# Long cross attention: a ring of seven PSUM banks in place of three behind the last peaks

## The chip, the cores and the metric

One core of one Trainium2 chip. The metric is the time of one execution on the device, in microseconds. Engines: PE is TensorE (matrix multiply; PEld are its weight loads), DVE is VectorE, ACT is ScalarE, POOL is GpSimd, SP starts DMAs. Matmuls write into PSUM, which has 8 banks of 512 float32 per partition; DVE and ACT read results from there.

## The reference, cut to what matters

A decoder of two layers on `x` (32 x 56 x 128) with a context `ctx_1024` (32 x 1500 x 128). Each layer is attention, cross attention and a mixture-of-experts feed-forward, each added to `x` after a layer norm. The change is in the cross attention of layer 1: 16 heads of dimension 8, with rotary embedding of queries and keys, over 1500 keys:

```python
q = _rope((x_query @ Wq.T) split into heads, T_q)
k = _rope((x_kv @ Wk.T) split into heads, T_k)
v = (x_kv @ Wv.T) split into heads
attn = softmax(einsum('bhqd,bhkd->bhqk', q, k) * SCALE)
out = einsum('bhqk,bhkd->bhqd', attn, v)
return out.transpose(0, 2, 1, 3).reshape(B, T_q, DIM) @ Wo.T
```

## The kernel before, in words

Six stages (`l0_attn`, `l0_xattn`, `l0_ffn`, `l1_attn`, `l1_xattn`, `l1_ffn`) run one after another. Every engine has its own program, and semaphores tie the programs together. The fifth, `l1_xattn`, is "long cross attention"; in the profiled execution it runs from about 600 to 1327 us, and its last score step starts at 1318.31.

**How the fifth stage is tiled.** It goes through the batches b = 0 to 31. The 1500 keys of a batch are 12 tiles (`NK`) of 125 (`KT`). A step is a tuple such as `("score", b, kt)`. The kinds that matter:

- `peak` (12 for a batch): two matmuls (L2147) into a pair of banks, and one DVE reduction (L2261) that takes the greatest score. It gives the shift of the softmax.
- `shift`, `halve`, `rest`, `full`: DVE reduces the peaks to one number for each row (L2267), ACT casts it twice (L2345, L2349), DVE takes the rest (L2271), PE transposes it (L2155), and DVE adds it to the queries (L2278). Scores then come out already shifted.
- `score` (12 for a batch): eight matmuls (L2170), four into each of two banks. ACT takes the exponential of each bank (L2341, 125 x 448 elements) into one of four buffers `Pb`.
- `apply` (12 for a batch): 32 matmul instructions for two steps (L2186), values times exponentials, always into bank 3, where the sum of a batch builds up.
- `own`: ACT copies bank 3 (L2355) when a batch is complete. `fold` (PE L2195, DVE L2286 and L2289) transposes and divides by the sums. `turn` (PE L2201, ACT L2361) transposes again. `out` (PE L2207, DVE L2295) projects and adds to `x`, for two batches at once. `norm` and `finish` (POOL L127, DVE L143, PE L151, ACT L156) are the layer norm for the next stage.
- `keys`, `blend`, `high`, `low`, `values`, `fetch`, `write`, `stack`, `mask` prepare later batches. There are none from batch 30 on.

**Order.** `order()` (L1947) is one list, written out by hand, that all five engines walk through in turn; each engine does its own part of a step, so each engine's order is fixed. The core is, for n = 12 b + kt:

```python
yield ("score", b, kt)
...peak steps of b + 1 (kt < 6) or b + 2 (kt >= 6)...
yield from short        # full, fold, turn, out, finish at odd kt
if n >= 3 and n % 2:
    yield ("apply", *divmod(n - 3, NK)); yield ("apply", *divmod(n - 2, NK))
```

So scores and applies come in pairs, and the applies belong to the two steps before the pair of scores just issued. The last peak of all is `("peak", 31, 11)`, in the step of `("score", 30, 5)`. The next step in the list is the score of (30, 6); 18 score steps are left from there. The small steps among them are `full` of batch 31, `turn` 29, `out` 14, `own` 30, `fold` 30, `finish` 14 and `turn` 30, in this order, and at the very end `own`, `fold`, `turn`, `out`, `norm` and `finish` of the last batch.

**Banks.** The loop at L2002 gives every step its banks before the programs are built. Peaks alternate between the pairs 4, 5 and 6, 7. Bank 3 belongs to the applies. Scores (two banks) and all the small steps (one) take theirs from the ring 0, 1, 2 in the order of the list. On PE each step waits until its banks are free: `free[bank]` holds the mark of whoever reads the bank last, for a score the exponential (`exped`), for a fold the division, and so on. On ACT the exponential of step n waits for its scores and for the apply of step n - 4 (`applied`), because of the four buffers.

**Next stage.** `l1_ffn` begins on PE with the router's 16 small products (L2490), when the last row of the layer norm is in place, and goes on with the experts (L916, L928). Its weights are loaded from the point of `("score", 30, 0)` on.

Of the kernel before, what the change touches and what calls it, by code (L numbers as in the profile page):

```python
# [14 lines left out]
B, S, D, H = 32, 56, 128, 16  # L15
# [44 lines left out]
def decoder(nc, a, out):  # L60
    with ExitStack() as ctx:
# [1766 lines left out]
        def l1_xattn():  # L1828
# [118 lines left out]
            def order():  # L1947
                yield from (("clear", 0), ("mask", 0), ("mask", 1), ("keys", 2, 0), ("keys", 2, 1))
                for k in range(12):
                    yield ("peak", 0, k)  # L1950
                    if k in (1, 3, 5):
                        yield ("blend", 2, k // 2)
                    if k == 1:
                        yield ("keys", 2, 2)
                    if k in (6, 9):
                        yield ("high", 2, k // 3 - 2)
                        yield ("low", 2, k // 3 - 2)
                yield from (("shift", 0), ("halve", 0), ("rest", 0), ("full", 0), ("mask", 2), ("high", 2, 2), ("low", 2, 2))
                yield from (("write", 2, 0), ("write", 2, 1))
                for i in range(6):  # L1960
                    yield ("stack", 2, i)
                for k in range(6):
                    yield ("peak", 1, k)
                for n in range(B * NK + 2):
                    b, kt = divmod(n, NK)
                    if n < B * NK:
                        yield ("score", b, kt)
                        if kt < 6 and b + 1 < B:
                            yield ("peak", b + 1, 6 + kt)
                        if kt >= 6 and b + 2 < B:  # L1970
                            yield ("peak", b + 2, kt - 6)
                    steps = side(b)[kt] if n < B * NK else []
                    short = [x for x in steps if kt % 2 and x[0] in ("full", "fold", "turn", "out", "finish", "query")]
                    yield from short
                    if n >= 3 and n % 2:
                        yield ("apply", *divmod(n - 3, NK))
                        yield ("apply", *divmod(n - 2, NK))
                        if kt == 1:
                            yield ("own", b - 1)
                    yield from [x for x in steps if x not in short]  # L1980
                yield from (("fold", B - 1), ("turn", B - 1), ("out", NT - 1), ("norm", NT - 1), ("finish", NT - 1))
# [17 lines left out]
                    f += [("fetch", 3, ch) for ch in range(3)]  # L1999
                return f  # L2000

            at, ring, pair = {}, 0, 0  # L2002
            for step in order():
                if step[0] == "peak":
                    at[step] = 4 + 2 * (pair % 2)
                    pair += 1
                elif step[0] in ("score", "query"):
                    at[step] = ring % 3, (ring + 1) % 3
                    ring += 2
                elif step[0] in ("keys", "values", "full", "fold", "turn", "out", "finish"):  # L2010
                    at[step] = ring % 3
                    ring += 1

            for t in range(NT + 4):
# [503 lines left out]
        for k, f in enumerate((l0_attn, l0_xattn, l0_ffn, l1_attn, l1_xattn, l1_ffn)):  # L2518
            place.update(used=stages[4].parts["passing"] if k == 5 else 0, low=k % 2 == 0 or k == 5)
            stages.append(f())  # L2520
# [136 lines left out]
```

## Time and profile before

| what | us |
|---|---|
| runs shown: median | 1519.72 |
| lowest, highest of 3 | 1514.0, 1524.32 |
| profiled execution: its time | 1509.65 |
| profiled execution: span of the trace | 1507.9 |
| busy in the span: PE, DVE, ACT, POOL | 1352.3, 1105.7, 820.5, 784.4 |
| first score step behind the last peak starts at | 1295.11 |
| last apply of the stage ends at | 1320.58 |

The span runs from the first to the last instruction of the trace; 1.75 us of the execution's time lie around it. The trace is of one execution, at the low end of the runs. Times in the rows are microseconds from the start of the span, unless marked ns. PEclk is the granted clock of TensorE as a share of 2.4 GHz.

### The profile page before, as it was taken

The numbers are of one execution on the slowest core, as the hardware profiler recorded it, in microseconds if no ns is written. First come the engines' busy times: TensorE is split into PE (matmuls) and PEld (weight loads), VectorE is DVE, ScalarE is ACT, GpSimd is POOL, SyncE is SP. The second block draws the span as 40 slices with busy tenths as digits, with TensorE's granted clock in tenths as the row PEclk, the third lists the DMA queues.
The fourth block names the chain that finished last, engine by engine and source line by source line (L and its number), as shares of the span: only waits on it lengthen the run. The fifth ranks groups of instructions, "written<-read, shape, count | busy, mean of one in ns | idle before, by whom it ended". The sixth has DMA issues, their size and how long they took to land.

```text
span 1507.9 us, 41832 instructions
## 1 busy us (share of the span) xinstructions
PE 1352.3 (90%) x17179; PEld 923.6 (61%) x17179; DVE 1105.7 (73%) x1832; ACT 820.5 (54%) x1804; POOL 784.4 (52%) x736
## 2 busy tenths in 40 slices
PE   6888999999979985769999999999999999789998
PEld 4557888788946662436656665666666566555554
DVE  6885767757768878648888888888888888335554
ACT  3442344356623431537777777777777777723332
POOL 6675322424676666727777777777777772000000
PEclk9878999999989998879999999999999999989999
DMA  4004400026214034464644464454455454204230
GB/s 129 2 2 130 159 2 2 18 79 192 62 30 72 22 51 94 96 122 122 133 120 130 116 135 123 124 125 127 123 129 130 120 130 105 65 11 104 62 62 13
DMA packets 77088, 134.71 MB, mean 89 GB/s; under 512 B 18081, under 2 KB 56867, under 8 KB 73635
## 3 DMA queue, kind: packets, MB, share of 16 engines
q1 hardware_dynamic: 74850, 127.84, 34.4%
q0 software_dynamic: 2048, 4.20, 0.9%
q8 instruction: 137, 2.24, 0.7%
q14 instruction: 53, 0.43, 0.1%
HBM read 100.54 MB, written 34.73 MB: 90 GB/s over the span
## 4 chain that ended last, share of the span: by engine, by line
PE 42%; ACT 10%; DVE 5%; issue 3%; POOL 1%; DMA 1%; SPq 0%; ACTq 0%; POOLq 0%; DVEq 0%
PE ps L2186 11%; PE ps L916 7%; PE ps L2170 7%; ACT ARENA L2341 4%; PE ps L928 4%; PE ps L2133 3%; PE ps L2124 3%; PE ps L2147 2%; DVE ARENA L2261 2%; ACT ARENA L2319 2%; ACT ARENA L2325 2%; ACT ARENA L2332 1%; PE ps L2195 1%; PE ps L2155 1%; DVE ARENA L2271 1%
## 5 line engine op out<-in xcount | busy, mean ns | idle before, releaser
L2261 DVE TENSOR_REDUCE ARENA<-ps 112x2 f32<-112x1000 f32 x384 | 456.7, 1197 | 116.0 <-PE ps L2147 109.2
L2341 ACT ACTIVATE ARENA<-ps 125x448 f32<-125x448 f32 x768 | 378.3, 549 | 136.6 <-PE ps L2170 135.7
L2391 POOL TENSOR_TENSOR ARENA<-ARENA 64x500 f32<-64x500 f32 x192 | 227.8, 1187 | 109.2 <-ACT ARENA L2319 90.3
L2170 PEld LDWEIGHTS ps<-ARENA 64*125 64x125 bf16 x3072 | 122.6, 134 | 134.4 <-ACT ARENA L2341 71.6
L2170 PE MATMUL ps<-ARENA 64*125 64x112 bf16 x3072 | 169.4, 229 | 20.5 <-ACT ARENA L2341 19.3
L2186 PE MATMUL ps<-ARENA 125*17 125x112 f32 x6144 | 185.6, 262 | 0.0
L127 POOL TENSOR_TENSOR rs<-rs,mhalf 128x1 f32<-128x1 f32 x96 | 73.3, 765 | 178.9 <-DVE rs L122 178.6
L2147 PE MATMUL ps<-ARENA 64*112 64x500 bf16 x768 | 152.7, 387 | 10.0 <-DVE ARENA L2261 9.7
L2186 PEld LDWEIGHTS ps<-ARENA 125*17 125x17 f32 x6144 | 136.8, 98 | 32.2 <-issue 21.9
L2402 POOL TENSOR_TENSOR ARENA<-ARENA 128x500 bf16<-128x500 f32 x96 | 129.3, 1348 | 44.7 <-ACT ARENA L2325 44.7
L2397 POOL TENSOR_TENSOR ARENA<-ARENA 128x500 f32<-128x500 f32 x96 | 122.1, 1272 | 18.0 <-DVE ARENA L2254 11.8
L2124 PE MATMUL ps<-ARENA 128*128 128x500 f32 x192 | 107.3, 642 | 14.7 <-DMA ARENA<-in_ctxT 13.8
L916 PE MATMUL ps<-XT,ARENA 128*128 128x448 f32 x288 | 116.9, 550 | 0.0
L2133 PE MATMUL ps<-ARENA 128*125 128x128 f32 x768 | 110.2, 287 | 0.0
L2133 PEld LDWEIGHTS ps<-ARENA 128*125 128x125 f32 x768 | 93.4, 190 | 23.9 <-issue 22.3
L916 PEld LDWEIGHTS ps<-XT,ARENA 128*128 128x128 f32 x288 | 55.7, 195 | 53.6 <-issue 53.6
L2254 DVE TENSOR_TENSOR ARENA<-ARENA 128x500 f32<-128x500 f32 x96 | 83.3, 867 | 4.9 <-ACT ARENA L2319 4.9
L2319 ACT COPY ARENA<-ps 128x500 f32<-128x500 f32 x96 | 55.7, 581 | 48.1 <-PE ps L2124 44.1
L1009 DVE TENSOR_TENSOR ARENA<-ps,ARENA 128x448 f32<-128x448 f32 x72 | 44.9, 623 | 42.0 <-PE ps L916 40.9
L156 ACT COPY XT<-ps 128x128 f32<-128x128 f32 x96 | 25.6, 271 | 81.9 <-PE ps L151 81.7
L2325 ACT CAST ARENA<-ARENA 128x500 bf16<-128x500 f32 x96 | 58.5, 610 | 21.0 <-POOL ARENA L2397 15.2
L789 POOL TENSOR_TENSOR ARENA<-ARENA 128x896 f32<-128x896 f32 x16 | 27.0, 1690 | 81.1 <-DVE ARENA L718 81.1
(273 smaller groups left out, 2394.9 us busy)
## 6 DMA issues: line engine op xcount, KB each, us to landing
ARENA<-key_parts SPq DMA_DIRECT2D x192, 187.5 KB, 3.7
ARENA<-in_ctxT SPq DMA_DIRECT2D x96, 250.0 KB, 3.6
key_parts<-ARENA SPq DMA_DIRECT2D x64, 375.0 KB, 2.6
ARENA<-token_weights SPq DMA_DIRECT2D x16, 512.0 KB, 5.2
slots<-in_c_blank SPq DMA_DIRECT2D x2, 1472.0 KB, 12.5
results<-ARENA SPq DMA_DIRECT2D x42, 64.0 KB, 3.2
ARENA<-in_L_ffn_W SPq DMA_DIRECT2D x1, 2048.0 KB, 8.6
ARENA<-in_L_ffn_W SPq DMA_DIRECT2D x4, 512.0 KB, 10.3
```

What stands on the lines that cost most here:

```text
L916: e.matmul(ps[:, bk, 0:448], wt(x, c), rhs, start=True, stop=True).then_inc(up_mm.sem, 1)
L2124: e.matmul(ps[:, b1, 0:500], wk, C[b % 3][:, 500 * ch:500 * ch + 500], start=True, stop=True) \
L2133: m = e.matmul(ps[0:KT, b1, 128 * k:128 * k + 128], C[b % 3][:, KT * kt:KT * kt + KT], wv, start=True, stop=True)
L2147: m = e.matmul(ps[0:112, b1 + h, 0:500], Q0[r, b % 3, g].rearrange("p j s -> p (j s)"), KS[b % 4][r, g, 500 * ch:500 * ch + 500], start=Tr ...
L2170: m = e.matmul(ps[0:KT, b1[h], 112 * g:112 * g + 112], KS[b % 4][r, g, KT * kt:KT * kt + KT], Q1[r, b % 2, 112 * g:112 * g + 112], start=T ...
L2186: m = e.matmul(ps[32 * c:32 * c + 17, 3, 112 * u:112 * u + 112], V[b % 3][0:KT, kt, x, :], Pb[0:KT, n % NP_, 112 * x:112 * x + 112], start ...
L2261: e.tensor_reduce(mxp[0:112, b % 2, 2 * g:2 * g + 2, ch], ps[0:112, b1:b1 + 2, 0:500], AX, ALU.max) \
L2325: e.copy(Kh[:, 500 * ch:500 * ch + 500], T1[:, (3 * b + ch) % 3, :]).then_inc(k_hi.sem, 1)
L2341: e.activation(Pb[0:KT, n % NP_, 448 * h:448 * h + 448], ps[0:KT, b1[h], 0:448], ACT.Exp, bias=0.0, scale=1.0).then_inc(exped.sem, 1)
L2391: e.tensor_tensor(T2[r:r + 64, :], T0[64 - r:128 - r, n % 2, :], sin[64 - r:128 - r, sl], ALU.mult) \
L2397: e.tensor_tensor(T1[:, n % 3, :], T1[:, n % 3, :], T2, ALU.add).then_inc(k_sum.sem, 1)
L2402: e.tensor_tensor(Kl[:, sl], T1[:, (3 * b + ch) % 3, :], Kh[:, sl], ALU.subtract).then_inc(k_lo.sem, 1)
```

## The change

Only the giving out of banks changes. From the score step (30, 6) on, the ring starts anew with seven banks, 0, 1, 2, 4, 5, 6, 7; before it, everything is as it was. Peaks are no longer in the list then. No instruction is added, removed or moved in any engine's order.

```diff
-            at, ring, pair = {}, 0, 0
+            at, ring, pair, banks = {}, 0, 0, (0, 1, 2)
             for step in order():
+                if step == ("score", B - 2, 6):
+                    ring, banks = 0, (0, 1, 2, 4, 5, 6, 7)
                 if step[0] == "peak":
                     at[step] = 4 + 2 * (pair % 2)
                     pair += 1
                 elif step[0] in ("score", "query"):
-                    at[step] = ring % 3, (ring + 1) % 3
+                    at[step] = banks[ring % len(banks)], banks[(ring + 1) % len(banks)]
                     ring += 2
                 elif step[0] in ("keys", "values", "full", "fold", "turn", "out", "finish"):
-                    at[step] = ring % 3
+                    at[step] = banks[ring % len(banks)]
                     ring += 1
```

The scores from (30, 6) on get the banks (0,1), (2,4), (5,6), (7,0), (2,4), (5,6), then for batch 31 (0,1), (2,4), (6,7), (0,1), (2,4), (5,6), (0,1), (2,4), (6,7), (0,1), (2,4), (5,6). Before, they were (0,1), (2,0), (1,2), (0,1), (0,1), (2,0), then (2,0), (1,2), (1,2), (0,1), (2,0), (1,2), (1,2), (0,1), (0,1), (2,0), (1,2), (0,1). The small steps take the banks between: `full` 31 bank 1 (before 2), `turn` 29 bank 7 (1), `out` 14 bank 5 (0), `fold` 30 bank 7 (0), `finish` 14 bank 5 (2), `turn` 30 bank 7 (2), and at the end `fold`, `turn`, `out`, `finish` banks 0, 1, 2, 4 (0, 1, 2, 0).

## Rows read from the trace of the kernel before

**Rows 1.** Stretch, us; busy PE, PEld, DVE, ACT, POOL; clock, DMA share, GB/s.

```profile
1200.00:1250.00 50.00, 47.64 (x824) 31.05 (x818) 43.03 (x55) 38.10 (x87) 37.71 (x32) 1.00 0.61 129
...
1295.10:1320.60 25.50, 18.40 (x481) 14.42 (x477) 3.05 (x14) 18.47 (x42) 0.60 (x1) 1.00 0.01 3
...
1320.60:1326.70 6.10, 2.12 (x9) 1.10 (x9) 2.14 (x9) 1.08 (x4) 0.60 (x1) 0.91 0.00 0
```

**Rows 2.** Who waited for whom, 1295.1 to 1320.7: total, times, longest.

```profile
PE ps L2170 <- ACT ARENA L2341: 6.9, 9, 0.8
...
ACT ARENA L2341 <- PE ps L2170: 6.2, 15, 1.1
...
PEld ps L2170 <- issue: 5.0, 9, 0.9
```

**Rows 3.** Timeline, one pair of steps: start us, us, engine and line.

```profile
1307.51 0.43 PE L2170 MATMUL ps<-ARENA 64*125 64x112 bf16 x8 [0.72 <-ACT ARENA L2341]
...
1307.87 0.96 PE L2186 MATMUL ps<-ARENA 125*17 125x112 f32 x32
...
1308.76 0.44 PE L2170 MATMUL ps<-ARENA 64*125 64x112 bf16 x8
...
1309.29 0.98 ACT L2341 ACTIVATE ARENA<-ps 125x448 f32<-125x448 f32 x2 [0.37 <-PE ps L2170]
...
1309.98 0.43 PE L2170 MATMUL ps<-ARENA 64*125 64x112 bf16 x8 [0.78 <-ACT ARENA L2341]
```

**Rows 4.** Timeline, start of the stretch.

```profile
1295.11 0.44 PE L2170 MATMUL ps<-ARENA 64*125 64x112 bf16 x8
...
1295.16 0.35 DVE L2289 TENSOR_TENSOR ARENA<-ps,ARENA 56x64 f32<-56x64 f32 x2
...
1297.98 0.20 ACT L2349 CAST ARENA<-ARENA 112x8 f32<-112x8 bf16 x1
...
1298.22 0.18 DVE L2271 TENSOR_TENSOR ARENA<-ARENA 112x8 f32<-112x8 f32 x1 [2.62 <-ACT ARENA L2349]
...
1299.24 0.57 PE L2155 MATMUL ps<-ident,ARENA 112*128 112x112 f32 x4
```

**Rows 5.** Timeline, end of the stretch.

```profile
1318.85 1.73 PE L2186 MATMUL ps<-ARENA 125*17 125x112 f32 x64
...
1319.67 0.21 ACT L2361 COPY ARENA<-ps 128x56 f32<-128x56 f32 x1
...
1320.69 0.35 ACT L2355 COPY ARENA<-ps 128x224 f32<-128x224 f32 x1 [0.81 <-PE ps L2186]
```

**Rows 6.** A group of the page (mean ns), then ACT's timeline with no wait.

```profile
L2341 ACT ACTIVATE ARENA<-ps 125x448 f32<-125x448 f32 x768 | 378.3, 549 | 136.6 <-PE ps L2170 135.7
...
1216.53 0.99 ACT L2341 ACTIVATE ARENA<-ps 125x448 f32<-125x448 f32 x2
...
1217.39 0.21 ACT L2345 CAST ARENA<-ARENA 112x8 bf16<-112x8 f32 x1
...
1217.91 0.98 ACT L2341 ACTIVATE ARENA<-ps 125x448 f32<-125x448 f32 x2
```

**Rows 7.** Timeline, the small matmul steps within the stretch.

```profile
1305.04 0.49 PE L2207 MATMUL ps<-ARENA 128*128 128x128 f32 x2
...
1310.35 0.62 PE L2195 MATMUL ps<-ident,ARENA 128*56 128x128 f32 x4
...
1313.38 0.33 PE L151 MATMUL ps<-ident,xn 128*128 128x128 f32 x1
...
1318.65 0.27 PE L2201 MATMUL ps<-ident,ARENA 56*128 56x56 f32 x1
```

**Rows 8.** Busy time by half microsecond: fall and rise of the clock.

```profile
1325.50:1326.00 0.50, 0.11 (x1) 0.14 (x1) 0.25 (x1) 0.15 (x1) 0.00 (x0) 0.63 0.00 0
...
1339.00:1339.50 0.50, 0.50 (x3) 0.28 (x2) 0.00 (x0) 0.00 (x0) 0.00 (x0) 0.72 0.00 0
```

**Rows 9.** Timeline, a score step at half clock.

```profile
611.63 0.67 PE L2170 MATMUL ps<-ARENA 64*125 64x112 bf16 x8
```

## The prediction

> **What bounds the kernel now.** I read the table of busy time by stretch first. Only the end of the fifth stage can change: the new bank list begins with the seventh score step of the last but one batch, 18 steps before the stage's end. In the middle of the stage PE is busy 47.6 of 50 us. In the 25.5 us from 1295.1 it is busy 18.4, ACT 18.5, DVE 3.1, POOL 0.6, and the DMA queues 1% [rows 1]. Nothing is full, so this is a chain between two engines. The list of waits for the same stretch says which: the scores on PE waited for the exponentials on ACT 6.9 us in 9 waits, and the exponentials for the scores 6.2 us in 15 [rows 2].
>
> The timeline of one pair of steps shows it in full [rows 3]. Call a score step S, the two exponentials of a step E, one apply step A. S starts at 1307.51, the two applies at 1307.87, the next S at 1308.76, its E at 1309.29, and only at 1309.98, 0.69 after E began, comes the second S, with 0.78 idle before it that an exponential ended. Three banks explain it: a score takes two, so a second score needs a bank that the first score's first exponential has emptied. The pair takes 0.89 (applies) + 0.53 (S to E) + 0.69 (E to the second S) + 0.36 (second S to the next applies) = 2.47 us. Nine pairs are 22.2 us; the small steps between them bring the stretch to 25.5 us: from the first S at 1295.11 [rows 4] to the end of the last applies at 1318.85 + 1.73 = 1320.58 [rows 5].
>
> **The change part by part.** It adds and removes no instruction; it changes in which bank 18 score steps and the eleven small steps from there on land. Cost of the code itself: nothing. What can change is when a bank is free. I followed the seven-bank list by hand. The three banks at the seam are the ones used now for the first score (0 and 1). The second score gets 2 and 4: bank 2 is emptied by the division at L2289, which runs from 1295.16 for 0.35 us, so it can start at about 1295.6; bank 4 held the last peak but one. That delay of 0.1 us is hidden by a longer wait below. After that every score takes banks whose reader, in the schedule below, is finished 0.5 us or more before, so no score or small step waits for a bank. Bank 3, where the applies accumulate, is untouched.
>
> Without bank waits two sums compete. ACT: a step's two exponentials last 0.99 together, but the next instruction starts 0.86 after their start (1216.53 to 1217.39) [rows 6], so 18 steps are 15.5 to 15.7, and the small ACT steps 0.52 (two casts, 1217.39 to 1217.91 [rows 6]), 0.35 (bank 3's copy) and 0.21 twice [rows 5], and some 0.27 for the transposed row, together 1.5: 17.2. PE: a pair costs 0.36 + 0.36 + 0.89 = 1.61 by the starts in [rows 3], nine are 14.5; the small matmul steps have 0.57, 0.62, 0.49, 0.33 and twice 0.27 [rows 4, 7], each 0.07 shorter to the next start as S and A are, together 2.1; the last two applies another 0.9: 17.5. The engines are level, so the order decides. I worked the order out, step by step, t from 1295.11: S starts only after the PE's last work and costs 0.37; E starts 0.53 after S, 0.87 after the previous E, and when the apply four steps back is done; A (0.445) needs the end of both exponentials, 0.98 after E's start, and about 0.12 for the signal (bank 3's copy starts 0.11 after the last apply [rows 5]).
>
> S0 0, E0 0.53; S1 0.49, E1 1.40; two applies 0.9 to 1.75; S2, S3 to 2.5. Here stands the one wait that the banks don't touch: the transposes at L2155 need the halves of the shift, which ACT casts only after E1 (from 2.27; last cast 2.57 to 2.77) and DVE subtracts, 0.18 us (now it is 1297.98 + 0.20, then 1298.22 + 0.18 [rows 4]). So the transposes start at 3.05, not at 2.5. Then applies 3.56 to 4.45, S4 4.45, E4 4.98 (ACT idles 0.5), S5 and the turn, applies to 6.28, S6, S7; the projection waits for ACT's copy after E5 (6.72 + 0.21), 7.03 to 7.44; applies to 8.33; S8, S9; the next applies wait for bank 3's copy (8.64 + 0.35), 9.10 to 9.99; S10, S11, fold, applies to 12.17; S12, S13, one transpose, applies to 14.06; S14, S15, applies to 15.69; S16, S17, turn, two applies to 17.52, one to 17.97. E17 starts at 17.29 and ends, with the signal, at 18.39; the last apply ends at 18.84.
>
> Now it ends at 25.47. So the stretch loses 6.6 us. Where it goes: 9 waits of about 0.75 before the second S (6.9 in all) and the wait for ACT at the end (before it four applies lie behind the last E for 0.8 us, after it one), less about 0.5 at the transposes and 0.4 for bank 3. What is late next is the applies behind the exponentials, and ACT itself. Low end of this term: 3 us, if an issue gap stands before each score (below). High end: 25.47 less the larger engine sum of 17.5 is 8.0.
>
> Behind the stretch the path is serial and not touched: bank 3's copy at 1320.69 [rows 5], fold, turn, projection, norm, two transposes. Its 6.1 us have PE busy 2.1 [rows 1], and then the router's matmuls start the last stage. All the weights of that stage are in: the queues move 3 GB/s in the stretch. So nothing waits for a DMA if PE comes 6.6 us earlier: the queues have been still for 25 us by then.
>
> TensorE's clock is the unknown. It was granted in full all through the stretch, fell to half in the half microsecond from 1325.5, 5 us after PE's dense work ended, and rose in the one from 1339.0 [rows 8], so 13.6 us at 1.2 GHz lie on the path. The sparse 6.1 us remain as long as they are, so I expect a fall at about the same place. Price by rows: a score's matmuls take 0.67 at half clock against 0.44 [rows 9, 3], and half a duration is the most there is to win. If fall and rise move by 3 us against the work, 1.5 us either way. I take 0.
>
> The Trainium skill speaks against the change: "TensorE: Matmul & The Clock Gate", section "A second HAM failure mode: psum-queue depth-cycling", reports a kernel that went round PSUM banks each iteration, where short idle times between groups made the clock go down and up. By that rule a ring of seven could bring half clock into the stretch; here the ring of three already goes round, with 0.78 us idle in each pair, and the clock stayed full, so the trace disagrees so far, and I leave the sum as it is.
>
> Sum: 1509.65 (profiled execution; its span is 1507.9) - 6.6 = 1503.0. That execution lies 10 us below the median of the three runs, 1519.72, which is the basis for a forecast of a median: 1519.72 - 6.6 = 1513.1. The three runs spread from 1514.0 to 1524.3, more than the effect.
>
> **The rivals.**
> Issue, not banks: PE's weight loads before the scores have 5.0 us idle in 9 waits under "issue" [rows 2]. If part of the 0.8 us is the sequencer's own, more banks don't remove it. For it: that row. Against: at the same places the matmul row names the exponential, and the start comes 0.69 after E's start, 0.55 for one exponential [rows 6] and 0.14 for the signal. Price: 0.18 before each of 18 scores, on PE, is 3.2 us; gain 3.4, time 1516.3.
>
> Nothing happens: the exponentials' four output buffers, or the applies behind the exponentials, hold the pair at 2.47 us. For it: two scores, then two applies, all in order, is a tight loop. Against: in the schedule the apply that E needs is done 0.9 us or more before. Gain 0 to 1, time 1519.2.
>
> Slower: the clock falls to 1.2 GHz within the stretch. Place: the wait for the transposes at t = 2.5 and the start of the pairs. By the score rows the matmuls take 1.52 times as long: PE's 17.5 become 26.6, and with 0.9 of waits 27.5 against 25.5, so 2.0 us slower, 1521.7; twice as long would be 35.9, 10 us slower. It decides from 1.4 times on, where 17.5 + 0.9 reaches 25.5. For it: the clock does fall 5 us after the dense work ends [rows 8], and the start of the stretch keeps its waits. Against: they are 0.5 us each, and PE gets denser, not sparser.
>
> The clock's low stretch moves: PE is denser before the serial end, the fall comes elsewhere. 1.5 us either way around the forecast, no case of its own.
>
> **How the numbers follow.** Forecast (gain 4.5 to 8) 0.73; issue 0.15; nothing 0.08; half clock in the stretch 0.04. No case reaches 1% (15 us, about what a measurement of this kernel can tell from no change) by itself; only the spread of the runs could show one. So same 0.96, faster 0.03, slower 0.01. For the range I take the forecast's own 1511.7 to 1515.2, extend it by the two small-gain cases to 1519, and by the runs' spread of 4 to 5 us downwards: 1507 to 1520.
>
> **What would show it.** Right: the last applies end about 18.9 us after the first S of the stretch; consecutive S of a pair start about 0.37 apart; the waits of S for the exponentials vanish from the list and applies or transposes wait instead; ACT busy near 17.5 of 19; four consecutive exponentials 0.43 apart. Wrong: S still starts 0.69 after E (a bank is still held), or 0.18 and more before each weight load; a granted clock under 1.00 before 1314; the fold after bank 3's copy later than 1315.5.

## The result and the profile after

The changed kernel took 1505.31 us, the median of 11 runs (1502.43 to 1511.19). The kernel before, run again beside it, took 1514.15 (1509.12 to 1524.32, 11 runs, among them the three shown above). The ratio is 0.9936, with a 95% interval of 0.9911 to 0.9961: 9.7 us less, between 5.9 and 13.5. The two medians are 8.8 us apart. As forecast, the change stays under 1%. The forecast time was 1513.1, with 1507 to 1520: the measured median is 1.7 us below the range.

The profiled execution has a span of 1500.6 us against 1507.9 before. Line numbers from L2003 on are 2 higher than before. The same view as [rows 1], by stretch from the first late score to the last apply and on:

```profile
1295.40:1314.00 18.60, 16.94 (x481) 13.17 (x477) 3.06 (x14) 16.94 (x42) 0.60 (x1) 1.00 0.01 4
1314.00:1320.10 6.10, 2.30 (x9) 1.17 (x10) 2.15 (x9) 1.08 (x4) 0.60 (x1) 0.81 0.00 0
1320.10:1345.00 24.90, 24.90 (x75) 15.89 (x76) 11.02 (x28) 7.01 (x12) 0.95 (x1) 0.77 0.00 1
```

The same 481 matmuls and 42 ACT instructions now stand in 18.6 us instead of 25.5; both engines are 91% busy. The serial end, from the last apply to the router, is as long as it was, 6.1 us. The list of waits of that stretch, against [rows 2]:

```profile
PEld ps L2172 <- issue: 1.7, 9, 0.2
ACT ARENA L2343 <- PE ps L2172: 1.6, 2, 1.1
PEld ps L2188 <- ACT ARENA L2343: 1.1, 2, 0.5
PEld ps L2157 <- DVE ARENA L2273: 0.8, 1, 0.8
```

The 6.9 us that scores waited for exponentials are gone. "Issue" before the weight loads of the scores fell from 5.0 to 1.7 us, in 9 waits each time, but not the same nine. Before, five of them stood in front of the second score of a pair, 0.82 to 0.88 us each, 4.3 us together: that was the bank wait under another name, and these five are gone. The other four were 0.18 us in front of a first score. Now every one of the nine pairs has that 0.18 in front of its first score. Two rows of before and one of after, PE's weight loads:

```profile
1307.48 0.33 PEld L2170 LDWEIGHTS ps<-ARENA 64*125 64x125 bf16 x8 [0.82 <-issue]
...
1308.76 0.31 PEld L2170 LDWEIGHTS ps<-ARENA 64*125 64x125 bf16 x8 [0.18 <-issue]
```

```profile
1305.27 0.54 PEld L2172 LDWEIGHTS ps<-ARENA 64*125 64x125 bf16 x16 [0.18 <-issue]
```

Left are one wait of the transposes for DVE (0.64 us), one of the projection for ACT's copy (0.41), and two of the last applies for the exponentials (0.29 and 0.30). The timeline, first at the transposes, then one pair in the middle, then the end (to be read against [rows 3 to 5]):

```profile
1295.41 0.89 PE L2172 MATMUL ps<-ARENA 64*125 64x112 bf16 x16
...
1297.96 0.20 ACT L2351 CAST ARENA<-ARENA 112x8 f32<-112x8 bf16 x1
...
1298.19 0.18 DVE L2273 TENSOR_TENSOR ARENA<-ARENA 112x8 f32<-112x8 f32 x1 [2.30 <-ACT ARENA L2351]
...
1298.42 0.60 PE L2157 MATMUL ps<-ident,ARENA 112*128 112x112 f32 x4 [0.64 <-DVE ARENA L2273]
...
1302.47 0.46 PE L2209 MATMUL ps<-ARENA 128*128 128x128 f32 x2 [0.41 <-ACT ARENA L2363]
...
1304.23 5.47 ACT L2343 ACTIVATE ARENA<-ps 125x448 f32<-125x448 f32 x12
...
1304.38 0.96 PE L2188 MATMUL ps<-ARENA 125*17 125x112 f32 x32
...
1305.27 0.67 PE L2172 MATMUL ps<-ARENA 64*125 64x112 bf16 x16
...
1312.54 0.58 PE L2188 MATMUL ps<-ARENA 125*17 125x112 f32 x16 [0.29 <-ACT ARENA L2343]
...
1313.41 0.58 PE L2188 MATMUL ps<-ARENA 125*17 125x112 f32 x16 [0.30 <-ACT ARENA L2343]
...
1314.11 0.35 ACT L2357 COPY ARENA<-ps 128x224 f32<-128x224 f32 x1 [0.65 <-PE ps L2188]
```

Two scores are now one row of 16 matmuls in 0.67 us, where they were two rows 1.2 us apart. ACT runs 12 exponentials in 5.47 us without a gap. The last apply ends at 1313.41 + 0.58 = 1313.99, 18.58 us after the first late score; I had forecast 18.84.

So the traces differ by 25.47 - 18.58 = 6.9 us in this stretch. The rest of the 7.3 by which the spans differ is small: the stretch began 0.3 later, and everything behind the last apply took 0.7 less. The whole-run comparison, though, says 9.7. That difference, and where the median of the kernel before lies, is what the experiments are about.

### The profile page after: what moved, and what is told of

It is laid out like the page before. It is cut to its first block, busy times and chain, and to the rows that moved or that the text cites. A ratio compares the mean times of both kernels' runs of the same rounds, so it can differ in the third digit from the quotient of the medians.

```text
span 1500.6 us, 41822 instructions
## 1 busy us (share of the span) xinstructions
PE 1348.9 (90%) x17179; PEld 920.0 (61%) x17179; DVE 1106.9 (74%) x1832; ACT 819.2 (55%) x1804; POOL 781.2 (52%) x736
## 4 chain that ended last, share of the span: by engine, by line
PE 42%; ACT 10%; DVE 5%; issue 3%; POOL 1%; DMA 1%; SPq 0%; ACTq 0%; POOLq 0%; DVEq 0%
PE ps L2188 11%; PE ps L916 7%; PE ps L2172 6%; ACT ARENA L2343 4%; PE ps L928 4%; PE ps L2135 3%; PE ps L2126 3%; PE ps L2149 2%; DVE ARENA L2263 2%; ACT ARENA L2321 2%; ACT ARENA L2327 2%; ACT ARENA L2334 1%; PE ps L2197 1%; PE ps L2157 1%; DVE ARENA L2273 1%
## 5 line engine op out<-in xcount | busy, mean ns | idle before, releaser
L2172 PE MATMUL ps<-ARENA 64*125 64x112 bf16 x3072 | 167.4, 228 | 13.2 <-ACT ARENA L2343 12.3
```

The costliest lines, as they stand in the source:

```text
L2172: m = e.matmul(ps[0:KT, b1[h], 112 * g:112 * g + 112], KS[b % 4][r, g, KT * kt:KT * kt + KT], Q1[r, b % 2, 112 * g:112 * g + 112], start=T ...
```

## The experiments

I compare intervals within each trace, since the start of the fifth stage alone moves by over 20 us between the traces (607 to 630 us). "Late" is from the last peak's matmul to ACT's copy of bank 3; it is 1.9 us longer than from the first late score to the last apply.

**The changed kernel once more.**

> The changed kernel once more. Theory: the whole gain is the shorter stretch from the first score step behind the last peak to the last apply of the stage (25.5 us before, 18.6 after) and what follows is as long as before, so 7 us, a ratio of 0.9954 to the kernel before. The profile should show that stretch at 18.5 to 18.7 again. Rival: the medians are 8.8 us apart because something before the stretch got faster too; then the ratio stays at or below 0.9942 and the stretch begins earlier than at 1295.

1517.95 us against 1527.9 for the kernel before beside it, ratio 0.9938 (0.9918 to 0.9958). Late 20.4 us, as in the first trace. So the stretch repeats exactly (18.58 us from first score to last apply, as in the first trace), the ratio stays on the rival's side, and the rival's sign for it (the stretch begins earlier) can't be read from single traces: the last peak came at 1311 instead of 1294, since this set of runs was slower in the first stages.

**Four banks.**

```diff
-                    ring, banks = 0, (0, 1, 2, 4, 5, 6, 7)
+                    ring, banks = 0, (0, 1, 2, 4)
```

> The late ring has banks 0, 1, 2, 4 only. Theory: what cost time was that a pair of scores needs four banks and had three; with four the second score no longer waits for the first exponential, though some scores now wait for the exponential two steps back. Stretch 19.0 to 20.5 us. Rival (it takes the full seven to gain, since the small steps eat banks too): 22 us or more.

First late score 1314.02, last apply 1334.78, so 20.8 us, late 22.6. One bank more gives 4.7 of the 6.9 us, a little less than expected (19.0 to 20.5). In its list of waits the scores wait for exponentials again, but little:

```profile
PEld ps L2172 <- ACT ARENA L2343: 2.7, 9, 0.5
...
PE ps L2172 <- ACT ARENA L2343: 1.2, 3, 0.4
```

1.2 us in 3 waits against 6.9 in 9 [rows 2]. All three stand before the second score of a pair that no small step separates from the pair before. There the second score gets exactly the two banks of the score two steps back, as the theory said: (30, 9) gets 2 and 4, which the exponentials of (30, 7) have to empty first. Behind a small step, which shifts the ring by one, no score waits; but four of the small steps wait for an exponential themselves, 1.6 us in all. One row of each kind:

```profile
1316.55 0.44 PE L2172 MATMUL ps<-ARENA 64*125 64x112 bf16 x8 [0.38 <-ACT ARENA L2343]
...
1319.88 0.27 PE L2203 MATMUL ps<-ident,ARENA 56*128 56x56 f32 x1 [0.46 <-ACT ARENA L2343]
```

The remaining 2.2 us are what the seven are for.

**Only the small steps apart.** The scores stay on banks 0, 1, 2, the small steps go round 4 to 7. `late` becomes true at the score step (30, 6), where the changed kernel starts its new ring; that line of the edit is left out here.

```diff
-                    at[step] = banks[ring % len(banks)]
-                    ring += 1
+                    if late:
+                        at[step] = 4 + small % 4
+                        small += 1
+                    else:
+                        at[step] = banks[ring % len(banks)]
+                        ring += 1
```

> The scores keep banks 0, 1, 2; only the small matmul steps (full, fold, turn, out, finish) get banks 4 to 7 from the score step (30, 6) on. Theory: nothing gained, because the second score of each pair still waits for the first exponential: stretch 25.0 to 25.5 us. Rival (the small steps' share of the ring was the cost): 22 us or less.

27.5 us, more than either expectation. The pairs are as before up to 1336, and then something else happens (timeline of PE and the half microseconds there, columns as in [rows 1]):

```profile
1333.73 0.43 PE L2176 MATMUL ps<-ARENA 64*125 64x112 bf16 x8 [0.78 <-ACT ARENA L2347]
...
1336.46 0.68 PE L2176 MATMUL ps<-ARENA 64*125 64x112 bf16 x8 [0.78 <-ACT ARENA L2347]
...
1337.07 1.70 PE L2192 MATMUL ps<-ARENA 125*17 125x112 f32 x32
```

```profile
1335.00:1336.00 1.00, 0.68 (x24) 0.36 (x12) 0.00 (x0) 0.59 (x3) 0.00 (x0) 1.00 0.00 0
1336.00:1336.50 0.50, 0.04 (x2) 0.07 (x3) 0.00 (x0) 0.50 (x2) 0.00 (x0) 0.94 0.00 0
1336.50:1337.00 0.50, 0.50 (x8) 0.47 (x8) 0.00 (x0) 0.25 (x1) 0.00 (x0) 0.50 0.00 0
```

The granted clock fell to half in the middle of the stretch, and 6.8 us of it ran at 1.2 GHz. The 0.78 us wait before the second score stands there as in the kernel before, so moving the small steps gains nothing (the theory), and the fall of the clock costs the 2 us by which this stretch is longer. This gave me a new theory: some executions of the three-bank stretch lose the clock, and that is a part of what the change gains.

**More traces of the kernel before.**

> The kernel before, for a second trace of it. Theory (the clock adds to the gain): three banks leave about 0.8 us idle before every second score, and in some executions the granted clock falls to half within the stretch behind the last peak; then the stretch (first score step to last apply) takes 27 to 28 us instead of 25.5. I expect this in one to three of the three traces. Rival: the fall seen in the run with only the small steps apart was an accident of that kernel; the stretch is 25.4 to 25.6 in all three, and the gain of the median beyond the 7 us is scatter.

> As before_2: a third trace of the kernel before. Stretch 27 to 28 us with half clock in it by the one theory, 25.4 to 25.6 by the other.

> As before_2: a fourth trace of the kernel before. Stretch 27 to 28 us with half clock in it by the one theory, 25.4 to 25.6 by the other.

Late 27.4 us in all three, no fall, where I had expected one to three. As far as these go, the rival is right.

**The kernel before against itself.**

> The kernel before timed against itself, to see what the comparison gives where nothing differs. Theory (the 2 us by which the medians say more than the traces are scatter): ratio 0.998 to 1.002, interval over 1. Rival (the second of two kernels run is favoured): ratio at or below 0.998 with 1 outside the interval. Stretch from the last peak's step to the copy of bank 3 as in the four traces before, 25.5 us from first score to last apply, if no half clock falls into it.

Ratio 1.000 (0.9976 to 1.0024), 1515.02 against 1514.38, so what runs second isn't favoured. But its trace had late at 30.3 us, with two falls in the stretch. The first one:

```profile
1307.00:1308.00 1.00, 0.92 (x9) 0.85 (x10) 0.00 (x0) 0.61 (x2) 0.00 (x0) 0.58 0.00 0
1308.00:1309.00 1.00, 1.00 (x18) 0.74 (x21) 0.49 (x2) 0.73 (x2) 0.00 (x0) 0.50 0.07 16
1309.00:1310.00 1.00, 1.00 (x26) 0.61 (x18) 0.70 (x4) 0.00 (x0) 0.42 (x1) 0.50 0.00 0
1310.00:1311.00 1.00, 0.67 (x12) 0.49 (x8) 0.00 (x0) 0.64 (x2) 0.18 (x1) 0.72 0.00 0
```

**The changed kernel, third time.**

> The changed kernel a third time. Theory (7.0 us from the stretch, and now and then 2 us more where the clock falls within the three-bank stretch): ratio 0.9948 to 0.9956. Rival (some 2 us more come from elsewhere): 0.9942 or less again.

1505.53 us against 1514.38, ratio 0.9942 (0.9921 to 0.9963). By the number that is the rival's "0.9942 or less"; the theory's 0.9948 to 0.9956 lies within the interval too, so this run doesn't decide. Late 20.4 again.

**Counting the falls, and provoking them.**

> A sixth trace of the kernel before, to count falls of the clock within its stretch behind the last peak. So far 2 of 6 three-bank traces had one (30.3 and 29.4 us from last peak to copy of bank 3, against 27.3 to 27.4 without), and 0 of 5 traces whose code there is the seven-bank one. Theory: about one in three again, 29 us or more when it happens. Rival: accidents of two runs; 27.3 to 27.4 in all that follow.

> As before_6: one in three with 29 us or more from last peak to copy of bank 3 by the theory, 27.3 to 27.4 by the rival.

> As before_6: one in three with 29 us or more from last peak to copy of bank 3 by the theory, 27.3 to 27.4 by the rival.

27.3 us in two of them, no fall. In before_6 it was 36.7: the clock fell at 1324 and the stretch ran at half clock for 27 us in all.

```profile
1318.00:1323.00 5.00, 3.65 (x96) 2.79 (x94) 2.99 (x6) 3.50 (x8) 0.00 (x0) 1.00 0.00 2
1323.00:1328.00 5.00, 4.22 (x72) 3.12 (x60) 0.80 (x2) 2.56 (x7) 0.00 (x0) 0.63 0.02 3
1328.00:1333.00 5.00, 3.43 (x60) 2.59 (x57) 0.00 (x0) 2.98 (x7) 0.00 (x0) 0.50 0.00 0
1333.00:1338.00 5.00, 4.28 (x66) 3.25 (x68) 1.20 (x5) 2.56 (x7) 0.60 (x1) 0.50 0.02 3
```

So 27 us at half clock made this stretch 9.4 us longer than 27.3. That execution took 1543.07 us, and the same kernel beside it 1534.11. The 9.0 between them is no proof of its own, since single executions of this kernel lie up to 15 us apart within one set (1509.12 to 1524.32 in the first).

**Two banks only.** This makes PE idle more.

```diff
-                    ring, banks = 0, (0, 1, 2, 4, 5, 6, 7)
+                    ring, banks = 0, (0, 1)
```

> The late ring has banks 0 and 1 only, so that every score waits for both exponentials of the one before and PE idles still longer. At full clock the pair should take 2.9 to 3.2 us instead of 2.47, 31 to 34 us from last peak to copy of bank 3. Theory (idle of PE in this stretch is what lets the clock fall): half clock for a good part of the stretch, and 34 us or more. Rival: the clock stays full and the time is 31 to 34.

Late 47.5 us, 41 of them at half clock, more than the 31 to 34 that were expected at full clock. The clock fell 4.5 us behind the first late score, after two waits of about 1.2 us. The timeline shows both parts: the second score waits 1.21 for both exponentials, and takes 0.67 instead of 0.44 itself.

```profile
1320.00:1330.00 10.00, 6.53 (x95) 4.74 (x93) 0.62 (x1) 3.89 (x9) 0.00 (x0) 0.50 0.00 0
1330.00:1340.00 10.00, 6.61 (x98) 4.95 (x99) 1.20 (x5) 4.50 (x10) 0.60 (x1) 0.50 0.01 2
```

```profile
1338.13 0.68 PE L2172 MATMUL ps<-ARENA 64*125 64x112 bf16 x8
...
1338.90 0.98 ACT L2343 ACTIVATE ARENA<-ps 125x448 f32<-125x448 f32 x2 [1.34 <-PE ps L2172]
...
1340.02 0.67 PE L2172 MATMUL ps<-ARENA 64*125 64x112 bf16 x8 [1.21 <-ACT ARENA L2343]
```

All traces together, in us:

| late ring | traces | last peak to bank 3's copy | falls in it |
|---|---|---|---|
| 0 and 1 | 1 | 47.5 | 1 |
| three banks for scores (before, small_apart) | 9 | 27.3, 27.4, 27.4, 27.4, 30.3, 36.7, 27.3, 27.3; 29.4 | 3 |
| 0, 1, 2, 4 | 1 | 22.6 | 0 |
| seven (after, seven_again, seven_3, router_ahead, tail_filled) | 5 | 20.4 to 20.5 | 0 |
| seven, transposes later (below) | 2 | 19.9 | 0 |

The mean of the nine is 28.9, and so is that of the eight of the kernel before alone. Against 20.4 the change saves 8.5 us in the mean of these traces, and 6.9 in an execution without a fall. The 8.5 is a rough number: 1.0 of its 1.6 us above 6.9 come from before_6 alone. Three comparisons of whole runs gave 0.9936, 0.9938 and 0.9942, which is 9.7, 9.5 and 8.8 us; both 8.5 and 6.9 lie within each interval. Taken together they give 9.3, with 1.9 either way (an estimate from the three intervals), which leaves 6.9 out. So the clock can explain the 2 us by which the comparisons exceed the stretch; that it does is not shown. Elsewhere the traces show no difference beyond their scatter: from the stage's first score to the last peak the nine three-bank traces take 683.9 to 689.5, the rest 684.2 to 688.7. The scatter of single traces is larger than the 2 us that are looked for.

The traces say more on where the clock falls. From 697 us to the last peak, 600 us of the same stage in which PE is hardly ever idle (47.6 of 50 us in [rows 1]), the clock is full in all 18 traces. It falls only behind the last peak.

**Can the clock be held in the serial end?** Sixteen extra matmuls in the shape of a peak go into PE's waits there; nothing reads what they write.

```diff
+                fill = {("fold", B - 1): 1, ("turn", B - 1): 2, ("out", NT - 1): 1, ("finish", NT - 1): 4}
                 for step in order():
+                    for _ in range(fill.get(step, 0)):
+                        for h, bk in enumerate((5, 7)):
+                            ...
+                            e.matmul(ps[0:112, bk, 0:500], Q0[...], KS[(B - 1) % 4][r, 0, 0:500], start=True, stop=True)
```

> Seven banks, and 16 extra matmuls of the shape of a peak (results unused) put into PE's waits in the serial end of the stage: 2 before the last fold, 4 before the turn, 2 before the projection, 8 before the layer norm's transposes. Theory: the clock falls because PE is sparse there; filled, it stays at 2.4 GHz through the router (6.96 us at half clock, 3.5 to 4.5 at full) and the first expert matmuls (8.5 us for 16, 6.0 at full): 4 to 6 us less than the changed kernel, less up to 0.5 for the chain being held up. Rival: the router's own products, of 8 columns each, let the clock fall whatever goes before: gain 2 us or less, or a fall a little later.

It came out as the rival said: 1524.54 against 1532.0, ratio 0.9943 (0.9918 to 0.9968), no better than the change alone (0.9936 to 0.9942). From bank 3's copy to the first expert matmul it took 11.5 us instead of 12.8.

```profile
1336.70:1342.50 5.80, 3.96 (x25) 1.74 (x24) 2.14 (x9) 1.06 (x4) 0.60 (x1) 1.00 0.00 0
1342.50:1343.50 1.00, 0.98 (x9) 1.00 (x10) 0.00 (x0) 0.00 (x0) 0.89 (x1) 1.00 0.00 0
1343.50:1345.00 1.50, 1.50 (x11) 1.50 (x10) 0.00 (x0) 0.00 (x0) 0.07 (x1) 0.60 0.00 0
1345.00:1348.00 3.00, 3.00 (x16) 3.00 (x16) 0.00 (x0) 0.00 (x0) 0.00 (x0) 0.50 0.03 5
```

In this trace the clock stayed full through the serial end, and then it fell at 1343.8 in the middle of the router's products, with PE shown busy all the time. Each of those is a load of 128 x 128 weights and a product of 8 columns. It fell 7.2 us behind the last apply; in the changed kernel without the fill it fell 1.7 to 4.3 us behind it. Whether the router's products or what was left of the idle time before them (PE was busy 3.96 of the 5.8 us) let it fall, this run doesn't separate.

**The router's products in those waits instead.**

```diff
+                ahead = {("fold", B - 1): 2, ("turn", B - 1): 5, ("out", NT - 1): 6, ("finish", NT - 1): 11}
                 for step in order():
+                    if step in ahead:
+                        stages[5].parts["route"](e, w, ahead[step])
                     pe_step(e, w, step)
```

`route(e, w, n)` issues the router's products up to row n - 1, with the waits they had.

> Seven banks, and 11 of the router's 16 products of the last stage are issued by PE in the waits of the serial end of the fifth stage (2 before the last fold, 3 before the turn, 1 before the projection, 5 before the two transposes of the layer norm). Theory: the end is a chain over DVE, ACT and POOL that leaves PE idle 4 of 6 us, so the products fit in and the router proper shrinks from 6.96 us to 5/16 of it, 2.2: 4.5 us gained over the changed kernel, if the clock falls and rises as it did. Rival: the products delay the chain by as much as they take, or the clock's rise moves back: gain 2 us or less.

1513.15 us against 1527.9, ratio 0.9903 (0.9877 to 0.9928), and 4.8 us below the changed kernel of the same set; bank 3's copy to the first expert matmul 8.9 us instead of 12.8 to 13.2: 4 us or a little more, near the 4.5 expected.

**The transposes later.**

```diff
-                    f[9].append(("full", b + 1))
+                    f[9 if b + 2 < B else 11].append(("full", b + 1))
```

> Seven banks, and the transposes of batch 31's shift stand one pair later in the order (at key tile 11 instead of 9 of batch 30). Theory: the one wait of 0.64 us at the transposes goes and ACT's idle 0.48 behind it shrinks; stretch (first score to last apply) 18.1 to 18.4 instead of 18.6, limited by ACT. Rival: the first score of batch 31 now waits for DVE's addition, 0.6 us, so 18.6 or more.

The wait is gone (the transposes follow the scores at 1303.06 with none), and late is 19.9 instead of 20.4, so 18.0 from first score to last apply, a little better than the theory's 18.1 to 18.4. What shows next is ACT, with eight exponentials in a row:

```profile
1301.91 3.58 ACT L2343 ACTIVATE ARENA<-ps 125x448 f32<-125x448 f32 x8
...
1303.06 0.60 PE L2157 MATMUL ps<-ident,ARENA 112*128 112x112 f32 x4
```

**Both.** The transposes later, 11 of the router's products ahead, and two more between the last two transposes of the layer norm.

> Seven banks, the transposes one pair later, and 13 of the router's 16 products issued in the waits of the serial end (11 as in router_ahead, 2 more between the last two transposes). Theory: 0.3 us from the transposes, 4.3 as measured for 11 products, 0.8 for the two more: ratio to before 0.9918 to 0.9925 (7.0 + 5.4 us). Rival: the two more delay the second transpose by what they save: 0.9925 to 0.993.

1500.64 us against 1514.38, ratio 0.9891 (0.9853 to 0.9929), the fastest of all and 4.9 us below the changed kernel of the same set. In its trace late is 19.9, and from bank 3's copy to the first experts 7.3 us instead of 12.8. The interval holds the expectation; it is too wide to tell theory from rival. By the traces the end is 1.6 us shorter than in router_ahead. Two things differ, and they are not separated: the two more products, and the fall of the clock, which came 4.5 us behind the last apply and not 1.9. The second varies by itself: in the three traces of the changed kernel the fall came 3.8, 1.7 and 4.3 us behind the last apply.

## Why the prediction was right and wrong

**The mechanism was right, and so was its size in a trace at full clock.** One stretch, its pair period, and the schedule worked out: 18.84 us forecast, 18.58 measured. The transposes waited as forecast (t = 3.05 forecast, 1298.42 - 1295.41 = 3.01 measured), the projection too (7.03 forecast, 7.06 measured), the last apply stood behind the last exponential, the serial end was unchanged. Four banks (4.7 of the 6.9 us) and the small steps alone (nothing) show that it is the banks of the scores. The forecast for the profiled execution itself was 1503.0; the one profiled after took 1502.43. Small misses: two scores in a row take 0.60 to 0.63 us up to the next applies, not 0.72, so a plain pair takes 1.49 and not 1.61; at the end two applies waited for exponentials, not one; and the small steps that take a bank in the late ring are ten, not eleven.

**The step that failed** is "the basis for a forecast of a median: 1519.72 - 6.6". I added a difference from one trace to a median of three runs. Over the 11 runs of the same set, those three among them, the kernel before has 1514.15: the basis was 5.6 us too high. That is most of the 7.8 us between forecast and result; the other 2.2 are the gain, 8.8 us between the medians where I had 6.6. Runs of one set spread over 15 us (1509.12 to 1524.32), and three of them don't place the median to 5 us. I allowed 4 to 5 us downwards, and the range ended 1.7 us above the result. The ratio that was measured would have put 1519.72 at 1510.0, inside the range.

Between sets it is worse: the same kernel had 1527.9, 1532.0 and 1514.4 later. The four later sets ran on four chips, one each, and nearly all of the difference is in front of the fifth stage: its first score starts at 607 to 616 us in the first set and on one of the four chips, and at 624 to 630 on the other three, with the same code there. Whether that is the chip or something else, no run here shows. It has no part in this miss, but it would in a forecast of a time for another set.

**The term that was probably mis-sized** is the clock. I had the granted clock as full "all through the stretch" and took 0 for it, from a single trace. Three of nine three-bank traces have half clock in it (two of the eight of the kernel before), for 6.8 to 27 us, which adds 1.6 us to the mean gain of the traces (28.9 less 27.3). That this is the missing 2 us is argued and not shown. The rival "slower: the clock falls to 1.2 GHz within the stretch" named the right mechanism and put it in the wrong kernel: it happened with three banks, and most with two, and not in the seven traces with seven. At the rate of three in nine, seven traces without a fall have a chance of some 6% (an estimate), so the traces make it likely that the change helps here, no more. My argument against the rival, "PE gets denser, not sparser", was the forecast of a gain that I didn't draw.

The page "TensorE: Matmul & The Clock Gate" of the Trainium skill, section "A second HAM failure mode: psum-queue depth-cycling", says that short idle times between groups of matmuls made the clock go up and down while a kernel went round its banks. Some executions here do show that, with 0.78 us idle in each pair and nothing longer before the fall. Going round banks was not enough for it: the ring of seven had no fall in seven traces, the ring of two 41 us of half clock in one. Read with these runs, the page's point on idle times speaks for this change, where I had read it as speaking against.

**The other rivals.** "Issue, not banks" fell: the issue idle of 0.82 to 0.88 us before second scores went with no instruction changed. The 0.18 us that stays before the first scores is idle time of the weight loads alone; the matmuls there show none. "Nothing happens" fell too. "The clock's low stretch moves" came out at the 0 that I took: the fall behind the stage came 3.8 us behind the last apply and not 5.0, and from bank 3's copy to the first experts it is 12.8 us against 12.9.

## What to carry to other kernels

Count the banks that two consecutive outputs need: here a pair of scores needs four, the ring had three, and the fourth alone gave two thirds of the gain. When an engine that sets TensorE's pace leaves short holes in its work, their price can be more than the holes, since some executions lost the clock there; one trace without a fall doesn't show that there is none. Forecast a difference or a ratio, and if a time has to be named, put the uncertainty of the kernel's own median on top; three runs don't bound it.

## What the runs showed of the hardware that I had not expected

In three of nine traces the clock fell in the stretch with three banks, where PE is busy about 70% (18.4 of 25.5 us in the trace of [rows 1]) and no hole before the fall was longer than 0.8 us; in none of seven traces did it fall in the stretch with seven banks, where PE is busy 91%. With the waits of the serial end partly filled, it fell in the router's products of 8 columns, with PE shown busy without a gap. Exponentials of 125 x 448 from PSUM are shown with 0.55 us each but follow one another every 0.45 (12 in 5.47 us). Idle under "issue" before a weight load can be a wait for a bank: 4.3 of the 5.0 us of before stood in five such waits, and they went with the banks.
